# Copies of q into the stacks moved to ScalarE's queue, with clears, barriers, the constant row and the counts moved

## What is computed

```python
x = x + xattn0(layernorm(x), ctx)      # 16 heads of 16; softmax over own keys and, apart, over
                                       # the context's keys; the two mixed by sigmoid(g) per head
x = x + ffn0(layernorm(x))             # 8 experts, 256 -> 512 -> 256, best one per row
x = x + xattn1(q=layernorm(x), ctx)    # one head of 256, softmax over 375 keys
x = x + ffn1(layernorm(x))             # 16 experts, 256 -> 1024 -> 256, 112 rows each at most,
                                       # rows placed in order of arrival, weighed by their gate
```

## Time and profile before

| what | value |
|---|---|
| median of 3 runs | 861.42 us (859.42 to 862.45) |
| the profiled execution | 867.99 us, span 866.0 us, mean granted TensorE clock 0.918 |
| busy: TensorE, VectorE, ScalarE, GpSimd | 736.7 us (85%), 432.2 (50%), 327.1 (38%), 213.1 (25%) |
| queue of SyncE (q1) | 86,102 packets, 110.85 MB, 61.1% of the 16 DMA engines' span |
| queue of ScalarE (q10) | 7,874 packets, 6.77 MB, 3.6% |
| `attention0` | 0 to 463.4 us |
| `ffn0` | 463.4 to 588.4 us |
| `attention1` | 588.4 to 735.4 us |
| `ffn1` | 735.4 to 866.0 us |

### The profile page before, as it was taken

The page is one execution under the profiler, slowest core; times in us unless marked ns, Lnnn a source line. Parts: engine busy times, 40 slices in busy tenths (PEclk is TensorE's granted clock), DMA queues, the critical chain, the costliest instruction groups (busy, mean ns, idle before and its releaser), DMA issues. The chain is left out here.

```text
span 866.0 us, 19102 instructions
## 1 busy us (share of the span) xinstructions
PE 736.7 (85%) x6340; PEld 543.1 (63%) x6341; DVE 432.2 (50%) x1316; ACT 327.1 (38%) x883; POOL 213.1 (25%) x362
## 2 busy tenths in 40 slices
PE   4689999999999999988874599974988874899996
PEld 2446666666666666665443266652766763899995
DVE  3356777777778777756722022212557754011111
ACT  2225555555555655544440133321344441011110
POOL 2302223332223223312100022222334432011111
PEclk9869999999999999999876599995889995799999
DMA  5989987788899888859333812205975581599970
GB/s 169 140 116 143 163 98 113 108 135 137 137 142 153 109 133 138 130 83 178 105 110 94 162 45 61 63 17 153 253 223 186 170 256 36 169 337 331 332 225 14
DMA packets 97877, 127.08 MB, mean 147 GB/s; under 512 B 23162, under 2 KB 82787, under 8 KB 97672
## 3 DMA queue, kind: packets, MB, share of 16 engines
q1 hardware_dynamic: 86102, 110.85, 61.1%
q0 software_dynamic: 3824, 8.46, 3.7%
q10 hardware_dynamic: 7874, 6.77, 3.6%
HBM read 74.68 MB, written 22.96 MB: 113 GB/s over the span
## 5 line engine op out<-in xcount | busy, mean ns | idle before, releaser
L473 ACT ACTIVATE probs<-psum 128x448 f32<-128x448 f32 (+2 forms) x256 | 128.6, 543 | 75.0 <-PE psum L761 73.6
L634 DVE TENSOR_REDUCE neg_max<-psum 112x2 f32<-112x750 f32 x128 | 119.3, 932 | 9.9 <-PE psum L744 8.6
L761 PE MATMUL psum<-stacks 102*128 102x112 bf16 (+1 forms) x1024 | 81.9, 218 | 10.6 <-DVE r_mine L982 5.3
L761 PEld LDWEIGHTS psum<-stacks 102*128 102x128 bf16 (+1 forms) x1024 | 58.7, 100 | 39.4 <-ACT probs L473 15.7
L744 PE MATMUL psum<-stacks 96*128 96x487 bf16 (+1 forms) x256 | 77.9, 387 | 2.0 <-DVE neg_max L635 0.9
L776 PE MATMUL psum<-probs,v 128*32 128x112 f32 (+2 forms) x2048 | 77.6, 269 | 0.0
L776 PEld LDWEIGHTS psum<-probs,v 128*32 128x32 f32 (+2 forms) x2048 | 45.8, 111 | 46.0 <-issue 30.7
L1889 PEld LDWEIGHTS psum<-e_xt,ring 128*128 128x128 f32 x512 | 62.3, 199 | 2.3 <-ACT e_xt L1836 1.4
L1889 PE MATMUL psum<-e_xt,ring 128*128 128x112 f32 x512 | 62.5, 283 | 0.9 <-ACT e_xt L1836 0.9
L1903 PE MATMUL psum<-ring,e_hid 128*112 128x256 f32 x256 | 57.9, 379 | 1.3 <-DVE e_hid L1863 1.3
L1856 DVE SCALAR_TENSOR_TENSOR e_y<-psum,e_x_in 112x256 f32<-112x256 f32 x16 | 7.7, 484 | 97.9 <-PE psum L1903 97.9
(11 more groups left out here) (226 smaller groups left out, 1397.8 us busy)
## 6 DMA issues: line engine op xcount, KB each, us to landing
ring<-in_L_ffn_w SPq DMA_DIRECT2D x32, 1024.0 KB, 8.1
stacks<-k_parts SPq DMA_DIRECT2D x96, 243.5 KB
ct_dram<-ct SPq DMA_DIRECT2D x16, 375.0 KB, 6.0
a_ct<-ct_dram SPq DMA_DIRECT2D x16, 375.0 KB, 4.4
a_ctx<-in_ctx SPq DMA_DIRECT2D x16, 375.0 KB
stacks<-q_parts SPq DMA_DIRECT2D x96, 56.0 KB
ctx_in<-in_ctx SPq DMA_DIRECT2D x16, 256.0 KB
w<-in_L_ffn_W SPq DMA_DIRECT2D x8, 512.0 KB, 11.6
```

Of the source, the lines that this page charges most:

```text
L473: nc.scalar.activation(probs[k % 4][0:keys, :, :], src, ACT.Exp, scale=DH ** -0.5).then_inc(s["exp_done"], 1)
L634: nc.vector.tensor_reduce(neg_max[:, 0, h:h + 2], psum[0:T, pair:pair + 2, 0:S], AX, ALU.max, negate=True)
L761: last = nc.tensor.matmul(bank[4 + k % 2][0:wide, j * T:(j + 1) * T], k_flat[n.third][:, first:first + wide], q_stack[n.third][:, h, :], s ...
```

## The change

Six things are moved, and nothing of the computation changes.

- The 6 DMAs a batch that bring q into its stack leave SyncE's queue. ScalarE issues them (`copy_q`), for batch b-1 in step b: at the head of the step in steps 1 and 2, and between the fourth and the fifth exponential in steps 3 to 16. They wait for GpSimd's third part of q.
- The eight copies of the inverse gates and the addition of the constant row on VectorE go from the end of step 1 to the end of step 2; `constant_row` on TensorE from the end of step 1 to step 2, behind its eight pairs.
- `r.count` on TensorE goes ahead of the keys of half 0.
- `place_rows` on VectorE goes ahead of the remainder of the keys of half 0.
- The two clears go from `ffn0`'s layout to ScalarE's steps of tiles 4 and 5.
- `phase` clears the semaphores of the stage before, ahead of one barrier, and the second barrier is gone.

```diff
--- before.py
+++ after.py
@@ -131,16 +131,16 @@
                 g.phase_sems.append(handle)
             return handle
 
-        g.phase_sems = None
+        g.phase_sems, g.used_sems = None, []
 
         def phase(run, *args):
 
             g.phase_sems = []
             run(*args)
+            if g.used_sems:
+                nc.clear_and_free_semaphores(g.used_sems)
             nc.all_engine_barrier()
-            nc.clear_and_free_semaphores(g.phase_sems)
-            nc.all_engine_barrier()
-            g.phase_sems = None
+            g.used_sems, g.phase_sems = g.phase_sems, None
 
         def dram(name, shape, dt=F32):
             return nc.dram_tensor(name, shape, dt, kind="Internal").ap()
@@ -301,8 +301,6 @@
                     rows = slice(DH * t, DH * t + DH)
                     if TERMS_K[t] == part:
                         sp.dma_start(k_stack[b.third][rows, :, :], k_parts[b.parity][:, part, :, :]).then_inc(s_stack[b.third], 16)
-                    if TERMS_Q[t] == part:
-                        sp.dma_start(q_stack[b.third][rows, :, :], q_parts[b.parity][:, part, :, :]).then_inc(s_stack[b.third], 16)
 
             def step(b):
                 if (b + 1).real():
@@ -457,14 +455,26 @@
                     act.wait_ge(s["wo_mm"], (n - 1).count(1, 1))
                 nc.scalar.copy(mixed[:, u, :], bank[6 + u][:, 0:T]).then_inc(s["mixed_ready"], 1)
 
+            def copy_q(n):
+                act.wait_ge(s["low_done"], n.count(2, 1))
+                if (n - 3).real():
+                    act.wait_ge(s["logits_mm"], (n - 3).count(16, 16))
+                for t in range(NT):
+                    rows = slice(DH * t, DH * t + DH)
+                    act.dma_start(q_stack[n.third][rows, :, :], q_parts[n.parity][:, TERMS_Q[t], :, :]).then_inc(s_stack[n.third], 16)
+
             def high_k(b, h):
                 nc.scalar.activation(k_parts[b.parity][:, 0, h, 0:S], bank[(0, 3)[h]][:, 0:S], ACT.Identity,
                                      bias=bias_t[:, h, 2:3]).then_inc(s["high_done"], 1)
 
             def step(b):
+                if (b - 1).real() and not (b - 3).real():
+                    copy_q(b - 1)
                 if (b - 3).real():
                     n = b - 3
                     for k in range(16):
+                        if k == 4 and (b - 1).real():
+                            copy_q(b - 1)
                         keys = T if k % 4 == 0 else CHUNKS[k % 4 - 1][1]
                         act.wait_ge(s["logits_mm"], n.count(16, k + 1))
 
@@ -591,6 +601,7 @@
                 dve.wait_ge(s["gate_step"], 3)
                 nc.vector.tensor_tensor(bv_mix[:, :], bv[0], bv[1], ALU.add).then_inc(s["bv_mix"], 1)
 
+            def gates_beside_values():
                 for p in range(2):
                     for c in range(NC + 1):
                         o = 0 if c == NC else 1
@@ -663,28 +674,26 @@
                 if b.real():
                     if (b - 1).real():
                         dve.wait_ge(s["low_done"], b.count(2))
-                    for h in (1, 0):
-
-                        if h == 1:
-                            dve.wait_ge(s["high_done"], b.count(6, 1))
-                        else:
-                            dve.wait_ge(s["high_done"], b.count(6, 6))
-                        rest_k(b, h)
-                        if h == 1:
-                            dve.wait_ge(s["high_done"], b.count(6, 5))
-                            rest_qk(b)
+                    dve.wait_ge(s["high_done"], b.count(6, 1))
+                    rest_k(b, 1)
+                    dve.wait_ge(s["high_done"], b.count(6, 5))
+                    rest_qk(b)
                 if (b - 4).real():
                     r.place_rows(dve, b - 4)
                     r.place_done(b - 4)
+                if b.real():
+                    dve.wait_ge(s["high_done"], b.count(6, 6))
+                    rest_k(b, 0)
                 if (b - 3).real():
                     n = b - 3
                     dve.wait_ge(s["wo_mm"], n.count(1, 1))
                     dve.wait_ge(s["xc_ready"], n.count(1, 1))
                     row = xs[:, n.at(), :].rearrange("t o d -> t (o d)")
                     nc.vector.tensor_tensor(row, bank[1][0:T, 0:D], row, ALU.add).then_inc(s["x1_ready"], 1)
-                if not b.looped() and b.c == 1:
+                if b.c == 1:
                     gates()
-
+                if b.c == 2:
+                    gates_beside_values()
                     dve.wait_ge(s["c_mm"], 1)
                     nc.vector.tensor_tensor(c_wide[:, :], bank[5][0:T, 0:D], c_wide[:, :], ALU.add).then_inc(s["c_ready"], 1)
 
@@ -811,6 +820,8 @@
                             turn(b - 3, 0)
                 if (b - 3).real():
                     values(b - 3, 14)
+                if b.c == 2:
+                    constant_row()
                 if b.real():
 
                     if (b - 2).real():
@@ -884,11 +895,12 @@
                                 last = nc.tensor.matmul(bank[2][:, (2 * h + o) * T:(2 * h + o + 1) * T], w_p[:, a_, 1 - o, h, :],
                                                         xt[b.parity][:, a_, :], start=(a_ == 0), stop=(a_ == 1))
                     last.then_inc(s["qk_mm"], 1)
+                if (b - 4).real():
+                    r.count(pe, b - 4)
+                if b.real():
                     if (b - 1).real():
                         pe.wait_ge(s["v_ready"], (b - 1).count(3, 1))
                     keys_of(b, 0)
-                if (b - 4).real():
-                    r.count(pe, b - 4)
                 if (b - 3).real():
                     n = b - 3
 
@@ -898,8 +910,6 @@
                     for h in range(2):
                         last = nc.tensor.matmul(bank[1][0:T, 0:D], mixed[:, h, :], wo[:, h, :], start=(h == 0), stop=(h == 1))
                     last.then_inc(s["wo_mm"], 1)
-                if not b.looped() and b.c == 1:
-                    constant_row()
 
             unrolled_steps(pe, step)
 
@@ -1193,11 +1203,6 @@
             act.wait_ge(s["setup_mm"], 4)
             nc.scalar.mul(g.u[:, :], bank[3][:, 0:2], D ** -0.5).then_inc(s["setup_copy"], 1)
             nc.scalar.copy(g.w_vo[:, :, :], bank[2][:, :].rearrange("p (k d) -> p k d", k=2)).then_inc(s["setup_copy"], 1)
-            per = E1 * C1 // P // 2
-            places = g.sorted1.rearrange("(q p k) (h n) -> q p (k h) n", q=2, p=P, h=2)
-            for part in range(2):
-                empty = g.empty[:, :].rearrange("p (o n) -> p o n", o=1).broadcast_to((P, 2 * per, ROW0))
-                act.dma_start(places[part], empty).then_inc(g.s_zero, 16)
             act.wait_ge(s["setup_copy"], SETUP)
             act.wait_ge(s["step"], TABLE)
             act.wait_ge(s["b1_made"], 1)
@@ -1326,10 +1331,18 @@
                             act.wait_ge(s["up"], (j - 2).count(1, 1))
                         nc.scalar.copy(xt2[j.parity][:, :, :], bank[2 + j.parity][:, 0:2 * P].rearrange("p (k t) -> p k t", k=2)).then_inc(s["x_copy"], 1)
 
+                    def clear_places(part, parts):
+                        per = E1 * C1 // P // parts
+                        places = g.sorted1.rearrange("(q p k) (h n) -> q p (k h) n", q=parts, p=P, h=2)
+                        empty = g.empty[:, :].rearrange("p (o n) -> p o n", o=1).broadcast_to((P, 2 * per, ROW0))
+                        act.dma_start(places[part], empty).then_inc(g.s_zero, 16)
+
                     lay_out_act(act)
                     copy_in(Item(0, 0, TILES))
 
                     def step(j):
+                        if not j.looped() and j.c in (4, 5):
+                            clear_places(j.c - 4, 2)
                         if (j + 1).real():
                             copy_in(j + 1)
                         if (j - 1).real():
```

## The result

The changed kernel took **941.44 us** in the median (938.22 to 945.11), the kernel before 861.93 beside it (859.42 to 867.51): ratio 1.092 (95% interval 1.088 to 1.096). The change costs 79.5 us where I forecast 27.7. The sign was right, the size was outside the range.

What follows compares the result with a forecast made beforehand. TensorE, nearly gapless in `attention0`'s repeated step, was taken as the bound. Terms 32.2 - 5.3 + 6.8 - 4.6 - 1.4 = +27.7 us gave a median of 889.1 us, range 872 to 908.

Steps and rivals of the forecast that it cites:

- ScalarE held by its issues: Steps 3 to 16: six q-copy issues, 3.84 us, stop ScalarE computing and delay exponential 4 and TensorE's product 6: +32.2 us.
- 2.3 us a step: Steps 3 to 16: product 6 2.15 us late, product 7 about 0.15 us more, over 14 steps.
- upper bound of 3.2: Steps 3 to 16: at 0.79 us an issue, 4.74 us for six, 3.2 us a step and 45 us in all.
- dearer issues: Rival: issues at 0.79 us give 902 us; lengthened further, or with the clock falling each step, 910 and more; chance 0.18.
- (e): Step 1: a 4.2 us TensorE pause may drop the clock to 1.2 GHz; +2 us taken (0 to 4).
- The wait for q's third part: Steps 3 to 16: waiting for GpSimd's third part costs nothing, since it is done 0.9 us before.
- Counts and places: Steps 5 to 16: TensorE's 0.44 us gap for `r_mine` goes, -5.3 us; no cost taken for the stream's sum.
- Steps 1 to 3: First steps of `attention0`: moves of issues, gates and constant row give +4.8, a possible clock fall +2, together +6.8 us.
- three signs that I named: Steps 1 to 3: ScalarE's copy 3.7 us late, L857 slower than 1.97 us, step 3 opening behind VectorE's `c_wide`.
- Clears: `ffn0`: first tile's wait shortened, -8.6 us, less +4 for late loads of tiles 6 to 9: -4.6 us (-8.6 to 0).
- Barriers: Stage ends: first stage's second barrier gone, -1.1 us, and about -0.3 for the later three: -1.4 us.
- The faster one (issues hide): Rival, `attention0` steps: SyncE's queue was the bound and ScalarE's issues hide, 851 us; chance 0.09.

Runs made afterwards that it cites:

- e1: The kernel before with only the q copies moved to ScalarE, nothing else of the change: 952.38 us, ratio 1.095.
- e3: The changed kernel with three of the six q copies on ScalarE and three on SyncE: 900.03 us, ratio 1.038.
- e7: The changed kernel with its six q copies issued one at a time, before every second exponential from 4 to 14: 891.97 us, ratio 1.022.
- e2: The changed kernel with the q copies back on SyncE's queue, all else as changed: 867.06 us, ratio 1.0005.
- e5: The changed kernel with q copies on SyncE, plus seven unused ScalarE copies between exponentials 3 and 4: 932.04 us, ratio 1.065.
- e9: The changed kernel with ten dummy TensorE products ahead of score product 6 of each step: 935.20 us, ratio 1.067.
- e11: The changed kernel with q copies on SyncE, plus three unused ScalarE copies between exponentials 3 and 4: 872.30 us, ratio 0.995.
- e8: The changed kernel with q copies on SyncE and clears in seven 0.5 MB parts, at tiles 0 to 5 and 18: 856.14 us, ratio 0.982.
- e13: The changed kernel with clears in seven parts and the q copies issued by GpSimd at the head of its step: 883.12 us, ratio 1.024.
- e12: The same kernel as e8 (q copies on SyncE, clears in seven parts), run in another submission: 855.11 us, ratio 0.976.
- e6: The changed kernel with twenty dummy TensorE products ahead of score product 6 in steps with q copies: 947.23 us, ratio 1.084.

## Why the prediction was right or wrong

**What bounds the kernel: right.** A microsecond taken from TensorE in the step was a microsecond of the kernel; e1 shows that the copies alone make the loss.

**ScalarE held by its issues: right; the term "2.3 us a step" was the step that failed.** The place, the direction and the engine that waits were as worked out. The price was not, by two parts:

- *The issues.* I took 0.64 us each, 3.84 for six, and measured 4.7. This makes the pause 3.15 us in place of 2.3, and it is within my upper bound of 3.2. Why they are dearer is open (e3, e7). That the longest issue on SyncE "came with its queue full", as I wrote there, is shown by no row.
- *The clock.* About 3.0 us a step, 30.25 - 24.08 - 3.15, which the sum did not have at all. Over 14 steps that is some 42 us of the 52 by which the forecast fell short; the issues make 12 and the clears 5 more, and the last two stages gave 3 back. That is a few microseconds too much, as the 14 steps are not all alike: over all of them the trace is 80.8 us longer than e2's, 5.8 a step, which leaves 2.6 for the clock. It stood only in a rival, "the 2.3 us pause brings the clock down in each step, 910 and more", with 0.18 together with dearer issues, and in term (e) for the one pause of step 1. In (e) I took it from the rows of a 7 us pause and was right (3.67 us for L868); for the pause that repeats 14 times I left it open because no row showed one. The evidence at hand was the same for both. What was missing was a price: a pause, and behind it products at the pace of 0.99 instead of 0.57 us for some 6.8 us, is 3 us more. e5, e9 and e11 confirm it from three sides: a pause made without DMAs brings it, filling the pause takes it away, and a pause of 0.5 us doesn't bring it.

**The wait for q's third part: right**, nothing waited there.

**Counts and places: right.** The 0.44 us wait went in every step (e2: 24.1 us steps), and the sum in the stream caused no new one.

**Steps 1 to 3: right in sum, partly by luck.** Step 3 starts 6.2 us later, and its first pair for the maximum, where I had counted 6.8, 5.4 us (70.85 against 65.49). The three signs that I named are there: ScalarE's copy late by 3.8 us (3.7 forecast), L868 at the slow clock, step 3 opening behind `c_wide`. But step 2's transposes came 5.1 us late (55.91 against 50.80) where my terms make 3.7, and the value products behind them gave 2.5 us back because they ran at the full clock, which they had not done before: eight in 1.96 us, 3.75 before. I had neither.

**Clears: wrong.** The head gained 8.2 us, nearly as forecast (8.6), but I charged 4 us for late tiles, spread over four of them. One tile came 6.56 us late, the products behind it ran at half speed (1.9 us more), and another was 0.91 late: 9.4 us, so the term is about +1 and not -4.6. Again the clock behind a pause was left out. The Trainium skill ("DMA: Bandwidth & Descriptors", section "Queues, rings and completion order") says that a DMA engine takes turns between its queues packet by packet. By that a small load should pass a large clear, and here as in the earlier trace rows it didn't: 9.9 us for a tile load beside clears of 1.8 MB, 4.7 of them lost ahead of its first packet. With clears of 0.5 MB (e8) TensorE waits for no tile behind the first.

**Barriers: small, as forecast.** The last two stages came out 3.5 us shorter, and I forecast 0.3. `attention1` alone varied between 143.0 and 147.5 us over the profiles, the two with the old barriers (before and e1) near the upper end with e8, so I read nothing into it.

**The rivals.** The faster one (issues hide) fell at the first step of the changed kernel, where exponential 4 comes behind 5.61 us of issues. But its core, that the copies could leave SyncE at no cost, was tried properly in e7 and e13, where the issues do hide in the middle steps, and it failed for another reason. The Trainium skill's rule that I had cited (the same page, "Issuing engines are not separate DMA queues": spreading saves only sequencer time) would make e13 equal to e12. They differ by 4.9% by the ratios (1.0235 / 0.9761) and by 3.3% by the times (883.12 / 855.11), so here moving copies to a second issuer cost something that this rule doesn't have.

## What to carry to other kernels

A DMA issue is work of the engine that issues it: put it where that engine's next result isn't wanted for as long as all the issues take, one at a time if the slack is short (e7: a loss of 9.2% became 2.2% by order alone). Where TensorE has no gaps, price a new pause of about three microseconds in each step at about twice its length, because the clock falls behind it; then look for pauses that are short enough not to bring it down. Cut bulk transfers that run beside small urgent loads into pieces: here 1.8 MB to 0.5 MB turned no gain into 11 us, 1.3%.

## What the runs showed of the hardware that I had not expected

- An issue of the same copy (256 pieces) took 0.56 us in the median one at a time on ScalarE (e7) and 0.53 on GpSimd (e13). Behind one another on ScalarE it took 0.65 in the median and 0.74 in the mean, at most 1.65 (after), and in e3 0.84 in the mean, at most 2.4.
- A pause of 2.9 us in a full stream brought TensorE's granted clock to 1.2 GHz in each step (e5), for 3.4 to 10.2 us in the changed kernel; one of 0.48 us did not (e11). In the middle steps of all traces every pause of 2.6 us or more was followed by such a stretch, and of the shorter ones some were and some weren't: 2.02 us in e13 was, 2.43 in e12 wasn't. Ten dummy products (2.44 us) in the pause kept the clock up.
- TensorE stops for up to 4.3 us with no semaphore to wait for when the q copies are issued outside SyncE's queue and its stream is otherwise full, 12 to 22 us in all between 90 and 450 us (e3, e6, e7, e9, e13). With all on SyncE it is 2 to 4 us. Where two kernels give TensorE the same program, the stops come at the same instructions (e7, e13), and all 54 in the traces end 1.2 to 2.1 us behind a 16 KB packet of the queue that the profile calls instruction.
- DMAs of 1.8 MB held 128 KB loads of another queue, 2.1 us as a rule, for 8.3 to 11.6 us (after, e2), and over half of the delay lay ahead of the load's first packet; those of 0.5 MB held none long enough to be waited for.
